# Two VectorE passes in place of three for normalised and modulated rows, in an adaLN attention-and-MLP kernel

## The reference, cut to what matters

```python
ada = t_emb @ w_ada + b_ada                       # one row of 6*256 numbers for each batch
sh_msa, sc_msa, g_msa, sh_mlp, sc_mlp, g_mlp = jnp.split(ada, 6, axis=-1)
xn = layer_norm(logmap0(x))
xm = expmap0(xn * (1 + sc_msa) + sh_msa)          # into q, k, v and the attention
...
x = mobius_add(residual, expmap0(attn_t))
xn = layer_norm(logmap0(x))
xm = expmap0(xn * (1 + sc_mlp) + sh_mlp)          # into the MLP
ff = plin(plin(xm, w_f1, b_f1), w_f2, b_f2)
ff_t = g_mlp * logmap0(ff)
return mobius_add(residual, expmap0(ff_t))
```

## Time and profile before

| | us |
|---|---|
| median of 3 runs | 1152.47 |
| lowest and highest | 1149.03, 1152.67 |
| the profiled execution's own time | 1151.27 |
| its span, first to last instruction | 1149.4 |
| busy: PE, DVE, ACT, POOL | 999.6, 964.9, 854.4, 551.0 |
| start of the attention's first DVE instruction | 384.66 |
| first norm pass of the MLP | 839.99 |

### The profile page before, as it was taken

How to read it: one execution, slowest core, us unless ns; L and a number is a source line. 1 busy time by engine, 2 the same in 40 slices (tenths; PEclk the granted TensorE clock), 3 DMA queues, 4 the chain that set the end, 5 groups by cost and what they waited for, 6 DMA issues and landing times.

```text
span 1149.4 us, 23488 instructions
## 1 busy us (share of the span) xinstructions
PE 999.6 (87%) x7666; PEld 647.6 (56%) x7688; DVE 964.9 (84%) x2211; ACT 854.4 (74%) x2322; POOL 551.0 (48%) x1009
## 2 busy tenths in 40 slices
PE   7999987887699279999999999999885688889876
PEld 7888873333355146666666666666552355455544
DVE  5888777999488867899998999999878799999983
ACT  3545548887797246888888888888778888888872
POOL 2344424554387432444444444444204576677763
PEclk9999998999599689999999999999997799999998
DMA  7111201341699643454554444442373555766634
GB/s 245 46 49 55 61 22 63 127 171 79 215 354 326 186 109 93 111 124 123 131 127 123 113 111 111 112 112 69 83 176 68 101 130 147 183 157 165 156 95 125
DMA packets 113676, 148.16 MB, mean 129 GB/s; under 512 B 9232, under 2 KB 99472, under 8 KB 112784
## 3 DMA queue, kind: packets, MB, share of 16 engines
q1 hardware_dynamic: 113008, 146.64, 46.8%
q10 hardware_dynamic: 544, 0.00, 0.0%
HBM read 111.22 MB, written 27.00 MB: 120 GB/s over the span
## 4 chain that ended last, share of the span: by engine, by line
PE 22%; issue 12%; ACT 12%; DVE 7%; POOL 6%; DMA 4%; SPq 2%; DVEq 0%; POOLq 0%; ACTq 0%
PE t_fB L2053 6%; POOL t_qk L1971 4%; PE t_bk L2022 4%; PE t_fA L2053 3%; PE t_bk L1386 3%; DMA t_qbd<-t_qt 3%; PE t_fB L1407 2%; SPq L1856 2%; ACT t_ysq L2192 1%; ACT t_junk L1425 1%; ACT t_vbd L1467 1%; ACT t_vbd L1451 1%; DVE t_qt L1619 1%; PE t_bk L2103 1%; ACT t_qt L2306 1%
## 5 line engine op out<-in xcount | busy, mean ns | idle before, releaser
L1386 PE MATMUL t_bk<-k_w12g,t_ut 128*128 128x512 f32 x256 | 126.3, 617 | 3.2 <-DVE t_y L1589 2.4
L412 POOL TENSOR_SCALAR s_hleak<-k_hs,k_leak 128x128 f32<-128x128 f32 x126 | 46.9, 372 | 96.2 <-ACT k_hs L367 96.2
L2053 PE MATMUL t_fA<-k_wqkv,t_ut 128*128 128x512 f32 (+1 forms) x256 | 91.2, 499 | 1.5 <-ACT t_ut L2162 1.5
L2053 PE MATMUL t_fB<-k_wqkv,t_ut 128*128 128x512 f32 (+1 forms) x256 | 90.9, 498 | 0.0
L285 PE MATMUL s_gsum<-k_hs,k_w0t 128*128 128x128 f32 x504 | 77.6, 297 | 6.8 <-ACT k_hs L367 0.8
L2022 PEld LDWEIGHTS t_bk<-t_qbd,t_kpar 64*128 64x128 f32 x1024 | 62.8, 189 | 31.6 <-ACT t_pt L2198 10.7
L2022 PE MATMUL t_bk<-t_qbd,t_kpar 64*128 64x128 f32 x1024 | 75.2, 287 | 6.2 <-DMA t_qbd<-t_qt 1.8
L1386 PEld LDWEIGHTS t_bk<-k_w12g,t_ut 128*128 128x128 f32 x256 | 50.4, 198 | 53.3 <-issue 49.6
L745 ACT ACTIVATE a_silu<-a_pg,k_wxscale 128x512 f32<-128x512 f32 x96 | 64.9, 694 | 17.5 <-PE a_pu L710 17.3
L285 PEld LDWEIGHTS s_gsum<-k_hs,k_w0t 128*128 128x128 f32 x504 | 65.6, 190 | 20.6 <-ACT k_hs L367 20.1
L364 ACT ACTIVATE s_gate<-s_gsum,k_b 128x128 f32<-128x128 f32 x128 | 40.1, 363 | 45.7 <-PE s_gsum L285 45.7
(11 more groups left out here) (388 smaller groups left out, 2910.1 us busy)
## 6 DMA issues: line engine op xcount, KB each, us to landing
t_scb<-g_rows SPq DMA_DIRECT2D x64, 256.0 KB, 4.8
t_shb<-g_rows SPq DMA_DIRECT2D x64, 256.0 KB, 5.9
...
```

The costliest lines, as they stand in the source:

```text
L1386: last = nc.tensor.matmul(z.fW[:, j, :], z.ut[:, c, j * P:(j + 1) * P], k["w12g"][:, c, :], start=False, stop=(c == C - 1))
L2053: last = nc.tensor.matmul(dst[:, w0:w1], ut[:, c, j * P:(j + 1) * P], k["wqkv"][:, c, w0:w1], start=(c == 0), stop=(c == C - 1))
```

## The change

In the MLP, `norm` now computes (x - mean) * scb, and `modulate` that times s plus shb, each as four `scalar_tensor_tensor` instructions of 256 elements; `shift` is gone. `scb` is thus needed by the first pass, and is free for the next load after it. Each row block of the second pass raises `u_ready` by itself, and ACT's `norms_u` waits block by block. At the start of the MLP the norm of group 1 moves behind `outputs(1)` and `gated`.

In the attention's group 0 the first pass moves into the norm chain, since it needs the mean but not s: two row blocks ahead of `vector_quotient`, one ahead of `vector_scale` and one ahead of `vector_norm`. The waits for `xf` and for `scb` move there too. The second pass stands where the three passes stood.

```diff
@@ norms_u, on ACT
-        act.wait_ge(s["u_ready"], g + 1)
         for j in range(GT):
+            act.wait_ge(s["u_ready"], g * GT + j + 1)
@@ modulate, on DVE
         dve.wait_ge(s["xh_ready"], (g + 1) * GT)
-        dve.wait_ge(s["sc_loaded"], (g + 1) * 32)
-        nc.vector.tensor_tensor(u, u, z.scb[:, :, :], ALU.mult).then_inc(s["um_ready"], 1)
+        dve.wait_ge(s["sh_loaded"], (g + 1) * 32)
+        for j in range(GT):
+            nc.vector.scalar_tensor_tensor(z.u[g % 2][:, j, :], z.u[g % 2][:, j, :], k["ln"][:, g * GT + j, 0:1], z.shb[:, j, :],
+                                           ALU.mult, ALU.add).then_inc(s["u_ready"], 1)
@@ norm, on DVE
+        dve.wait_ge(s["sc_loaded"], (g + 1) * 32)
         for j in range(GT):
-            nc.vector.tensor_scalar(z.u[g % 2][:, j, :], z.x1_row(g, j), k["ln"][:, g * GT + j, 0:1], k["ln"][:, g * GT + j, 1:2],
-                                    ALU.mult, ALU.add).then_inc(s["xh_ready"], 1)
-
-    def shift(self, g):
...
-        nc.vector.tensor_tensor(u, u, z.shb[:, :, :], ALU.add).then_inc(s["u_ready"], 1)
+            nc.vector.scalar_tensor_tensor(z.u[g % 2][:, j, :], z.x1_row(g, j), k["mv"][:, g * GT + j, 0:1], z.scb[:, j, :],
+                                           ALU.subtract, ALU.mult).then_inc(s["xh_ready"], 1)
@@ second_scale, on SP
-                sp.wait_ge(*((zs["um_ready"], g) if g else (s["um_ready"], NG)))
+                sp.wait_ge(*((zs["xh_ready"], g * GT) if g else (s["um_ready"], NG)))
@@ start of the attention, on DVE
+            def first_rows(j):
+                nc.vector.scalar_tensor_tensor(u[:, j, :], xf[:, j, :], k["mv"][:, j, 0:1], scb[:, j, :], ALU.subtract, ALU.mult).then_inc(s["xhat_ready"], 1)
+
             scales.vector_squares(dve)
+            dve.wait_ge(s["xf_loaded"], 16)
+            dve.wait_ge(s["sc_loaded"], 32)
+            first_rows(0)
+            first_rows(1)
             scales.vector_quotient(dve)
+            first_rows(2)
             scales.vector_scale(dve)
+            first_rows(3)
             scales.vector_norm(dve)
@@ the second pass of group 0 of the attention
-            dve.wait_ge(s["xf_loaded"], 16)
+            dve.wait_ge(s["sh_loaded"], 32)
             for j in range(GT):
-                nc.vector.tensor_scalar(u[:, j, :], xf[:, j, :], ln_of(0, j, 0), ln_of(0, j, 1), ALU.mult, ALU.add).then_inc(s["xhat_ready"], 1)
-            modulate(0)
-            dve.wait_ge(s["um_ready"], 1)
-            dve.wait_ge(s["sh_loaded"], 32)
-            nc.vector.tensor_tensor(u[:, :, :], u[:, :, :], shb[:, :, :], ALU.add).then_inc(s["u_ready"], 1)
+                dve.wait_ge(s["xhat_ready"], j + 1)
+                rows = nc.vector.scalar_tensor_tensor(u[:, j, :], u[:, j, :], ln_of(0, j, 0), shb[:, j, :], ALU.mult, ALU.add)
...
```

More of the change, by code:

```diff
@@ L1244 @@
              "la", "rn", "n", "e", "l1", "inv", "ld", "iden", "rsy", "xs", "w", "om", "den", "th", "top", "k", "A", "B")
-MLP_SIGNALS = ("sc_loaded", "sh_loaded", "gb_loaded", "xin_loaded", "stored", "xh_ready", "um_ready", "u_ready",
+MLP_SIGNALS = ("sc_loaded", "sh_loaded", "gb_loaded", "xin_loaded", "stored", "xh_ready", "u_ready",
                "un_ready", "act_u", "su_ready", "us_ready", "utp_ready", "ut_ready", "w_ready", "quad_ready", "guard_ready", "act_q", "s1_ready",
@@ L1552, in modulate @@
     def modulate(self, g):
-        nc, dve, z, s = self.nc, self.dve, self.z, self.s
-        u = z.u[g % 2]
+        nc, dve, k, z, s = self.nc, self.dve, self.k, self.z, self.s
         dve.wait_ge(s["xh_ready"], (g + 1) * GT)
-        dve.wait_ge(s["sc_loaded"], (g + 1) * 32)
-        nc.vector.tensor_tensor(u, u, z.scb[:, :, :], ALU.mult).then_inc(s["um_ready"], 1)
+        dve.wait_ge(s["sh_loaded"], (g + 1) * 32)
+        for j in range(GT):
+            nc.vector.scalar_tensor_tensor(z.u[g % 2][:, j, :], z.u[g % 2][:, j, :], k["ln"][:, g * GT + j, 0:1], z.shb[:, j, :],
+                                           ALU.mult, ALU.add).then_inc(s["u_ready"], 1)
     def quads(self, g):
@@ L1660, in norm @@
             dve.wait_ge(t["ln_b"], 1)
+        dve.wait_ge(s["sc_loaded"], (g + 1) * 32)
         for j in range(GT):
-            nc.vector.tensor_scalar(z.u[g % 2][:, j, :], z.x1_row(g, j), k["ln"][:, g * GT + j, 0:1], k["ln"][:, g * GT + j, 1:2],
-                                    ALU.mult, ALU.add).then_inc(s["xh_ready"], 1)
-    def shift(self, g):
-        nc, dve, z, s = self.nc, self.dve, self.z, self.s
-        u = z.u[g % 2]
-        dve.wait_ge(s["um_ready"], g + 1)
-        dve.wait_ge(s["sh_loaded"], (g + 1) * 32)
-        nc.vector.tensor_tensor(u, u, z.shb[:, :, :], ALU.add).then_inc(s["u_ready"], 1)
+            nc.vector.scalar_tensor_tensor(z.u[g % 2][:, j, :], z.x1_row(g, j), k["mv"][:, g * GT + j, 0:1], z.scb[:, j, :],
+                                           ALU.subtract, ALU.mult).then_inc(s["xh_ready"], 1)
 def attention_mlp(nc, dr, k, out):
@@ L1814, in second_scale @@
             def second_scale(g):
-                sp.wait_ge(*((zs["um_ready"], g) if g else (s["um_ready"], NG)))
+                sp.wait_ge(*((zs["xh_ready"], g * GT) if g else (s["um_ready"], NG)))
                 second_rows(z.scb, 4, g, "sc_loaded")
             def second_shift(g):
-                sp.wait_ge(*((zs["u_ready"], g) if g else (s["u_ready"], NG)))
+                sp.wait_ge(*((zs["u_ready"], g * GT) if g else (s["u_ready"], NG)))
                 second_rows(z.shb, 3, g, "sh_loaded")
@@ L2436, in turn @@
                     once(second.modulate, 0)
-                    once(second.shift, 0)
                     outputs(0)
-                    once(second.norm, 1)
                     outputs(1)
                     gated()
+                    once(second.norm, 1)
+                    outputs(2)
                     once(second.modulate, 1)
-                    outputs(2)
-                    once(second.shift, 1)
                     outputs(3)
@@ L2524, in _ @@
             dve.wait_ge(s["ln_x"], 1)
-            dve.wait_ge(s["xf_loaded"], 16)
+            dve.wait_ge(s["sh_loaded"], 32)
             for j in range(GT):
-                nc.vector.tensor_scalar(u[:, j, :], xf[:, j, :], ln_of(0, j, 0), ln_of(0, j, 1), ALU.mult, ALU.add).then_inc(s["xhat_ready"], 1)
-            modulate(0)
-            dve.wait_ge(s["um_ready"], 1)
-            dve.wait_ge(s["sh_loaded"], 32)
-            nc.vector.tensor_tensor(u[:, :, :], u[:, :, :], shb[:, :, :], ALU.add).then_inc(s["u_ready"], 1)
+                dve.wait_ge(s["xhat_ready"], j + 1)
+                rows = nc.vector.scalar_tensor_tensor(u[:, j, :], u[:, j, :], ln_of(0, j, 0), shb[:, j, :], ALU.mult, ALU.add)
+                if j == 0:
+                    rows.then_inc(s["um_ready"], 1)
+            rows.then_inc(s["u_ready"], 1)
             second.split_bias(flat_o[0:1, 0:3 * D], flat_ot[0:1, 0:3 * D // 2].bitcast(BF16))
@@ L2553, in _ @@
                 once(second.modulate, i)
-                once(second.shift, i)
                 if i in gates:
```

## The result

The changed kernel takes **1162.61 us** (median of 4 runs, 1160.51 to 1164.33) beside 1152.57 for the kernel before: a ratio of 1.0091, 95% interval 1.0068 to 1.0114. It is about 10.5 us slower. The prediction was 1154.3 with a range of 1149 to 1159, and it gave "slower" 0.23. It was wrong.

What follows compares the result with a forecast made beforehand. It took the late MLP turns to be bound equally by DVE's own work and a two-turn PE-DVE-ACT loop, with the attention's start delaying everything. Terms +3.5 - 0.4 - 1.3 = +1.8 on 1152.47 gave 1154.3 us, range 1149.0 to 1159.0.

Steps and rivals of the forecast that it cites:

- (a), the start: Attention's start: new rows wait for `scb`, POOL's memset holds a `tensor_scalar`, so the passes end 3.5 us later.
- rival 3: Attention's start: the memset doesn't hold the chain, so the start costs only +1.0, giving 1151.8 us; chance 0.1.
- (b), sizes of the instructions: MLP turn on DVE: first pass +0.29, one 1.58 pass for `modulate` and `shift` -0.81, together -0.52 us.
- rival 4: The new DVE instructions run at half rate: +32 us, giving 1186 us; chance 0.02.
- rival 2: `scb` comes late in the MLP, 0.5 us in each of 13 turns, giving 1160.8 us; chance 0.15.
- (b), the loop: MLP: the two-turn loop over PE, DVE and ACT grows by 0.29 from 30.76 to 31.05 us.
- (b), turns 7 to 10: MLP turns 7 to 10: DVE bounds there, so the 0.52 saved a turn counts, -2.1 us in four turns.
- (c), POOL beside DVE: Small POOL instructions beside DVE's passes wait only for short instructions, some 0.5 us each: -1.3 us.
- (d): Hidden work: `scb` free sooner, finer `u_ready`, new DVE order at the MLP's start: 0, bounds -0.5 and +0.5 us.
- The sum: Whole kernel: +3.5 for the attention's start, -0.4 for the MLP's turns, -1.3 for POOL, together +1.8 us.

Runs made afterwards that it cites:

- attn_only: Kernel before with only the attention's first group changed to two passes, the MLP keeping its three; 1152.86 us, ratio 1.0011.
- mlp_warm: mlp_only plus twelve useless PE transposes in `turn_u`, ahead of its wait for ACT; 1146.43 us, ratio 0.9950.
- before_long_first: Kernel before plus one useless DVE `tensor_tensor` of 256 elements right behind `norm`; 1161.09 us, ratio 1.0084.
- before_warm: Kernel before plus twelve useless PE transposes between `turn_xd` and `turn_u`, nothing of the change; 1148.23 us, ratio 0.9975.
- after_warm: The whole change plus twelve useless PE transposes between `turn_xd` and `turn_u`; 1149.97 us, ratio 0.9984.
- mlp_only: Kernel before with only the MLP changed to two passes, the attention's first group keeping its three; 1158.86 us, ratio 1.0056.
- short_first: mlp_only with the first pass as four `tensor_scalar`, leaving out the multiplication by `scb`; 1152.74 us, ratio 1.0012.
- before_late2: Kernel before, three passes, with only its first pass moved behind `gated`; 1150.73 us, ratio 0.9980.
- mlp_fill: mlp_only plus one useless DVE instruction (about 0.6 us) behind the second pass from group 2 on; 1160.71 us, ratio 1.0068.

## Why the prediction was wrong, point by point

- **(a), the start: right.** 3.3 us against 3.5, by the mechanism named (the wait for `scb`, the memset that holds the `tensor_scalar`); rival 3 falls. (The three old passes took 5.97 us from 392.35 to 398.32, not the 3.4 that the text has; the sum doesn't use the 3.4.) Whether the attention took up a part is not settled: behind a start of 17.11 it lasted 451.4 to 453.6, behind 13.8 it lasted 451.8 to 455.1, and attn_only as a whole lost 1.3 us. The Trainium skill, "SBUF — State Buffer", section "Who interferes with whom", says that DVE instructions with two SBUF inputs contend with a POOL instruction that reads SBUF and not with one that only writes, and that `tensor_scalar` can take the shared ports; the new rows' 0.88 us and line 1153's 2.40 beside the same memset agree.
- **(b), sizes of the instructions: right.** `norm` and `modulate` take 1.58 us each with a pitch of 0.395 (1032.70 to 1034.28, and 1024.27 to 1025.85); rival 4 falls. `scb` never came late in the MLP (in the trace of after no first pass waits for its load), so rival 2 falls, though a loss near its size came.
- **(b), the loop: this step failed.** It took 31.05 us for two turns, made of PE, DVE and ACT durations read in the one stretch of the trace where PE restarts at full speed. Measured: 34.0, and 31.2 only where useless transposes keep the restarts at full speed (mlp_warm). I had the right loop and even the right edit to suspect (+0.29 inside, -0.81 outside), but priced the 0.29 at 0.29, as if the loop could only be 0.29 longer. before_long_first measured it at about 10 us for the whole kernel.
- **(b), turns 7 to 10: wrong.** I expected -2.1 because DVE bounds there. From the modulation of group 6 to that of group 10 it was 65.74 us before and 66.22 after: DVE, which waited for nobody there before, now waits 2.9 us for PE (at 948.50, 979.58 and 981.51), so it no longer bounds. The pauses ahead of `turn_u` grew from 2.40 and 2.66 us to 3.40 and 3.64, and 1000.35 is slow as 1002.56 was. The clock is not all of it: with full-speed restarts the same stretch took 65.73 (before_warm) and 65.28 (after_warm), -0.5 and not -2.1.
- **(c), POOL beside DVE: right.** At the same place as the earlier trace rows ACT's wait for POOL fell by 1.36 us, against the 1.3 of the sum (whose own terms, 2.39 less 2 x 0.5, give 1.4), and from group 2's `turn_u` to group 3's it is 21.30 us after and in mlp_only, 22.41 before and in attn_only, so 1.1 us of it reached PE:

```profile
889.59 0.20 ACT L2228 ACTIVATE t_s_ld<-t_s_den 128x4 f32<-128x4 f32 x1 [1.19 <-POOL t_s_den L1934]
```

- **(d): right as far as seen**; nothing new waits there.
- **The sum** of +1.8 lies close to what after_warm against before_warm shows (+1.0 to +1.7), in part by luck, as said above. What was missing is a rival of its own: "PE's pause becomes longer or comes in every second turn, and its restarts are slow", at 2.7 us each; with three to seven more of them, by estimate, 8 to 19 us. It would have stood on the two slow `turn_u` of the trace of before. After has five such restarts from group 4 on, three more than before.

**What stays open:** which restart is slow. The length of the pause right ahead of it does not tell. In attn_only pauses of 2.30 and 2.31 were followed by a slow and a fast one, in short_first those of 3.29 and 3.30 (the lines are attn_only's):

```profile
1033.40 1.94 PE L1369 MATMUL t_fA<-k_ident,t_xf 128*128 128x128 f32 x8 [2.30 <-ACT t_xf L1497]
...
1065.54 1.06 PE L1369 MATMUL t_fA<-k_ident,t_xf 128*128 128x128 f32 x8 [2.31 <-ACT t_xf L1497]
```

and before_late2 has a slow one behind 0.89 and 0.99 with `turn_xd` between, while a single pause of 1.82 in each turn was never followed by one in the kernel before (lines of before_late2):

```profile
1047.34 1.06 PE L1398 MATMUL t_fB<-k_ident,t_qbd 128*128 128x128 f32 x8 [0.89 <-POOL t_qbd L1351]
1049.39 1.84 PE L1369 MATMUL t_fA<-k_ident,t_u 128*128 128x128 f32 x8 [0.99 <-ACT t_u L1497]
```

This may be why mlp_fill has one run at 1153.45 among six from 1157.65 to 1162.60: there, I take it, the turns got out of the lopsided order, but no trace shows it.
